# An attention and FP4 passage on one core: gates term by term, a fourth scaling buffer, earlier unpacking, and a reordered start

## The reference

```python
x = (h - mu) * rsqrt(var + EPS) * ln_g + ln_b
q, k, v = (x @ w.T + b for w, b in ...)        # 16 heads of 128, rope on q and k
attn = softmax(where(causal, -inf, q @ k.T * scale))
y = (attn @ v) @ wo.T + bo + residual
Wg, Wu, Wd = (LUT[4-bit codes] * scales per 32) # MLP 2048, the FP4 weights
gate, up = xt @ Wg.T, xt @ Wu.T
out = (gelu(gate) * up) @ Wd.T
```

## Time and profile before

| | before |
|---|---|
| median of 3 runs | 573.86 us (573.19 to 574.56) |
| profiled execution, its own time | 574.48 us |
| its span, first to last instruction | 572.7 us |
| busy: PE, DVE, ACT, POOL | 529.3, 472.8, 388.4, 389.3 us |
| granted clock of TensorE, mean | 0.994 |

### The profile page before, as it was taken

The page is one execution under the profiler, slowest core; times in us unless marked ns, Lnnn a source line. Parts: engine busy times, 40 slices in busy tenths (PEclk is TensorE's granted clock), DMA queues, the critical chain, the costliest instruction groups (busy, mean ns, idle before and its releaser), DMA issues.

```text
span 572.7 us, 11429 instructions
## 1 busy us (share of the span) xinstructions
PE 529.3 (92%) x4176; PEld 360.9 (63%) x4176; DVE 472.8 (83%) x875; ACT 388.4 (68%) x856; POOL 389.3 (68%) x351
## 2 busy tenths in 40 slices
PE   6768999999999999999997989899999989999894
PEld 2445666666666666766665555455688778656673
DVE  6899999999999999999998786576636986867656
ACT  5965879689787787778788576657676457557221
POOL 6877898899999899889897588622324453534442
PEclk9998999999999999999999999999999999999998
DMA  8235484646554335675355324112110000000002
GB/s 267 76 68 112 120 166 94 124 103 140 94 126 86 72 73 88 156 132 70 70 94 134 106 85 136 38 49 83 31 38 2 2 1 1 0 1 2 2 1 73
DMA packets 97880, 44.63 MB, mean 78 GB/s; under 512 B 87712, under 2 KB 90144, under 8 KB 97824
## 3 DMA queue, kind: packets, MB, share of 16 engines
q1 hardware_dynamic: 97392, 43.61, 33.5%
q10 hardware_dynamic: 432, 0.29, 0.2%
HBM read 21.86 MB, written 1.05 MB: 40 GB/s over the span
## 4 chain that ended last, share of the span: by engine, by line
PE 53%; DVE 22%; ACT 8%; POOL 7%; issue 6%; DMA 2%; SPq 1%; ACTq 0%; POOLq 0%; DVEq 0%
PE bank L1700 47%; PE bank L1887 4%; DVE turned L1244 3%; POOL qkl L647 2%; DVE parts L1267 2%; DVE nmax L1232 2%; DMA x<-in_x 2%; DVE stats L1114 1%; DVE turned L1475 1%; DVE stage L1516 1%; DVE ol L1281 1%; DVE w_all_l L1179 1%; DVE nrm L1127 1%; PE bank L1747 1%; ACT bank L838 1%
## 5 line engine op out<-in xcount | busy, mean ns | idle before, releaser
L1700 PE MATMUL bank<-xTh,w_all_h 128*128 128x512 f16 (+2 forms) x388 | 128.6, 331 | 12.3 <-DVE w_all_l L1179 3.6
L1700 PE MATMUL bank<-xTh,w_all_l 128*128 128x512 f16 (+2 forms) x388 | 128.5, 331 | 0.0
L1700 PE MATMUL bank<-xTl,w_all_h 128*128 128x512 f16 (+2 forms) x388 | 128.3, 331 | 0.0
L647 POOL TENSOR_TENSOR qkl<-turned,qkh 128x512 f16<-128x512 f32 (+1 forms) x44 | 55.4, 1260 | 96.0 <-ACT qkh L980 95.7
L571 POOL TENSOR_TENSOR rr<-turned 64x512 f32<-64x512 f32 x62 | 87.3, 1408 | 12.2 <-DVE turned L1244 8.3
L572 POOL TENSOR_TENSOR rr<-turned 64x512 f32<-64x512 f32 x62 | 82.2, 1326 | 3.6
L838 ACT ACTIVATE bank<-bank,nmax 128x128 f32<-128x128 f32 (+3 forms) x128 | 63.9, 499 | 29.8 <-DVE nmax L1232 29.0
L1244 DVE SCALAR_TENSOR_TENSOR turned<-bank,small,rope 128x1024 f32<-128x1024 f32 x64 | 81.1, 1269 | 0.6 <-PE bank L1768 0.6
L980 ACT ACTIVATE qkh<-turned 128x512 f16<-128x512 f32 (+1 forms) x44 | 27.6, 628 | 60.6 <-DVE turned L1475 60.6
L1267 DVE SCALAR_TENSOR_TENSOR parts<-bank,rscaled,parts 128x128 f16<-128x128 f32 (+3 forms) x128 | 64.3, 540 | 1.5 <-ACT parts L849 1.5
L1700 PEld LDWEIGHTS bank<-xTh,w_all_h 128*128 128x128 f16 (+1 forms) x388 | 37.9, 98 | 40.5 <-issue 11.0
(11 more groups left out here) (240 smaller groups left out, 1480.1 us busy)
## 6 DMA issues: line engine op xcount, KB each, us to landing
stage<-in_per_head SPq DMA_DIRECT2D x16, 512.0 KB, 4.3
xa<-in_codes SPq DMA_DIRECT2D x32, 128.0 KB, 2.8
stage<-in_packed SPq DMA_DIRECT2D x12, 256.0 KB, 3.0
stage<-in_scales SPq DMA_DIRECT2D x12, 256.0 KB, 3.5
pT<-parts SPq DMA_TRANSPOSE x128, 2.9
stage<-in_w1T SPq DMA_DIRECT2D x2, 512.0 KB, 4.7
rope<-in_ropes SPq DMA_DIRECT2D x1, 512.0 KB, 8.2
x<-in_x SPq DMA_DIRECT2D x1, 512.0 KB, 9.1
```

The costliest lines, as they stand in the source:

```text
L647: pool.tensor_tensor(il[n % 2][0:rows, :], inter[0:rows, n % 2, :], ih[n % 2][0:rows, :], ALU.subtract).then_inc(g_il, 1)
L1700: last = pe.matmul(dst, l, r, start=start and i == 0, stop=stop and i == 2, skip_group_check=skip)
```

## The change

- First heads. The norm of batch OTHER that the residual needs leaves `norms0`; its three instructions stand at steps 5, 6 and 7 (LATE_NORM_AT). GpSimd no longer waits for d_qkl ahead of its two weight halves, only ahead of the rotation. The copy of the turned x of OTHER into xT moves from VectorE to ScalarE (in `high_xT0`). VectorE makes the late weight half of a step ahead of `low_xT0`.
- Loads. Packed codes and scales are loaded apart; packed 4 to 7 at steps 25, 26, 28 and 29, scales 4 to 7 after the last `turn`. Bytes 4 and 5 are made at step 31.
- Passage. w32 has four buffers. VectorE copies the first 256 columns of piece 0 (`high_fp4_first`) at step 31, ScalarE the rest at step 32. TensorE makes gates 0 and 1 term by term at step 32 (`gates_high` ahead of `out_project(30)`, `gates_low` behind), then ups 0 and 1, and in step 33 gate 2, up 2 and gate 3; the loop over tiles begins with up 3. Pair 2 is unpacked ahead of `low_fp4(2)`, and `scaled(4)` and `scaled(5)` stand ahead of `low_inter(0)`. The later pieces stand at other tiles, and the shift and normal_x of batch FIRST one tile sooner.

The diff, cut (new semaphores, three-part `norm0`, signatures left out; all instructions that move are there):

```diff
@@ -37,7 +37,9 @@
...
 BYTES_AT = (23, 24, 25, 27)
+PACKED_AT = (25, 26, 28, 29)
 X0_TURN_AT = {0: 0, 1: 1}
+LATE_NORM_AT = (5, 6, 7)
@@ -54,9 +56,9 @@
...
 Q_PIECES = 3 * MLP // Q_COLS
-UNPACK_AT = {2: 3, 4: 4, 7: 5}
-SCALED_AT = {0: 4, 1: 5, 3: 6, 4: 7, 5: 8, 6: 9, 8: 10, 9: 11}
-HIGH_AT = {0: 3, 1: 4, 2: 5, 4: 6, 5: 7, 6: 8, 7: 9, 9: 10, 10: 11}
+UNPACK_AT = {1: 3, 4: 4, 6: 5}
+SCALED_AT = {2: 6, 3: 7, 4: 8, 6: 9, 7: 10, 8: 11}
+HIGH_AT = {0: 4, 1: 5, 3: 6, 4: 7, 5: 8, 7: 9, 8: 10, 9: 11}
@@ -196,7 +198,7 @@
...
-w32 = [rope, rr, turned[:, 1, 2:4, :]]
+w32 = [rope, rr, turned[:, 1, 2:4, :], turned[:, 1, 0:2, :]]
@@ -467,12 +472,17 @@
...
-    def load_fp4(j):
+    def load_packed(j):
+        w, cols = q_piece(j)
+        if j >= 4:
+            sp.wait_ge(a_byte, j - 3)
+        sp.dma_start(raw[:, j % 4, :], packed[w, :, cols]).then_inc(s_raw[j % 4], 16)
+
+    def load_scales(j):
...
             sp.wait_ge(g_w32, NIBBLES * (j - 3))
-        sp.dma_start(raw[:, j % 4, :], packed[w, :, cols]).then_inc(s_raw[j % 4], 16)
-        sp.dma_start(scl[:, j % 4, :], scales[w, :, cols]).then_inc(s_raw[j % 4], 16)
+        sp.dma_start(scl[:, j % 4, :], scales[w, :, cols]).then_inc(s_scl[j % 4], 16)
@@ -495,9 +505,6 @@
...
     for s in STEPS:
-        if s == UNITS - 1:
-            load_fp4(4)
-            load_fp4(5)
@@ -509,9 +516,17 @@
...
             for j in range(4):
-                load_fp4(j)
-    for j in range(6, Q_PIECES):
-        load_fp4(j)
+                load_packed(j)
+                load_scales(j)
+        if s in PACKED_AT:
+            load_packed(PACKED_AT.index(s) + 4)
+    for j in range(4, 8):
+        load_scales(j)
+    for j in (8, 10):
+        load_packed(j)
+        load_packed(j + 1)
+        load_scales(j)
+        load_scales(j + 1)
@@ -560,13 +575,19 @@
...
         pool.wait_ge(d_rope, 2 * u + 2)
+        if u - 2 == LATE_NORM_AT[0]:
+            pool.wait_ge(g_var0, 5)
+        if u - 2 == LATE_NORM_AT[1]:
+            pool.wait_ge(g_var0, 6)
+        if u - 2 == LATE_NORM_AT[2]:
+            pool.wait_ge(g_norm0, 3)
...
             pool.wait_ge(d_qkl, 2)
-            pool.wait_ge(g_norm0, 3)
+            pool.wait_ge(g_norm0, 2)
@@ -617,30 +641,31 @@
...
         norm0(1, OTHER, square0[:, :], (1.0 + LN_EPS) / D, LN_EPS ** 2)
-        norm0(2 + OTHER, OTHER, square0[:, :], 1.0 / D, LN_EPS)
...
         if s == 0:
-            pool.wait_ge(d_qkl, 2)
...
             low_qk(s + 1)
+        if s in LATE_NORM_AT:
+            norm0(2 + OTHER, OTHER, square0[:, :], 1.0 / D, LN_EPS, (LATE_NORM_AT.index(s),))
...
         pool.wait_ge(d_bits, 2 * (j // 2) + 2)
-        if j >= 3:
-            pool.wait_ge(d_fl, j - 2)
+        pool.wait_ge(s_scl[j % 4], 16 * (j // 4 + 1))
+        if j >= 4:
+            pool.wait_ge(d_fl, j - 3)
...
             code = bits_of(j // 2)[:, c, j % 2, :].bitcast(FP8)
-            pool.tensor_tensor(w32[j % 3][:, c, :], code, scl[:, j % 4, :], ALU.mult).then_inc(g_w32, 1)
+            pool.tensor_tensor(w32[j % 4][:, c, :], code, scl[:, j % 4, :], ALU.mult).then_inc(g_w32, 1)
@@ -677,7 +702,7 @@
...
     pool.wait_ge(g_qkl, lows_of(UNITS, 0) - 1)
-    for j in range(4):
+    for j in range(6):
         scaled(j)
@@ -801,7 +826,10 @@
...
         for c in cs:
-            act.wait_ge(d_xT, place(b) * KC + c + 1)
+            act.wait_ge(t_xT, place(b) * KC + c + 1)
+            act.activation(xT[:, c, :], acc_bank[c][:, :], ACT.Identity,
+                           scale=ln_g[:, c:c + 1], bias=ln_b[:, c:c + 1]).then_inc(a_xT, 1)
+            act.wait_ge(a_xT, c + 1)
@@ -881,6 +909,9 @@
...
             high_o(s - 2)
+        if s == UNITS - 1:
+            to_bytes(4)
+            to_bytes(5)
@@ -929,10 +960,15 @@
...
+    def high_fp4_rest():
+        act.wait_ge(g_w32, NIBBLES)
+        act.activation(fh[0][:, :, 2 * P:Q_COLS], w32[0][:, :, 2 * P:Q_COLS], ACT.Copy,
+                       scale=W_SCALE * FP4_AS_FP8).then_inc(a_fh, 1)
...
         act.wait_ge(g_w32, NIBBLES * (j + 1))
-        act.activation(fh[w][:, :, cols], w32[j % 3][:, :, :], ACT.Copy, scale=W_SCALE * FP4_AS_FP8).then_inc(a_fh, 1)
+        act.activation(fh[w][:, :, cols], w32[j % 4][:, :, :], ACT.Copy, scale=W_SCALE * FP4_AS_FP8).then_inc(a_fh, 1)
@@ -997,6 +1033,7 @@
...
             gate_of(0, ACT.Gelu_apprx_tanh)
+            high_fp4(3)
@@ -1004,20 +1041,16 @@
...
             high_xT(1, 0, (1,))
-            act.wait_ge(t_proj, 2 * UNITS)
-            high_fp4(0)
...
             act.wait_ge(t_v, UNITS)
+            high_fp4_rest()
...
     def between_first(m):
-        if m == 0:
-            to_bytes(4)
-            to_bytes(5)
...
             normal_y(0, 1)
-        if m == 11:
+        if m == 10:
             normal_x(0, 1)
@@ -1190,9 +1222,9 @@
...
     dve.wait_ge(d_vec, 1)
-    turned_x0(FIRST, (1,))
+    turned_x0(1)
     dve.wait_ge(a_xTh, 1)
-    turned_x0(FIRST, (0,))
+    turned_x0(0)
@@ -1307,11 +1339,9 @@
...
             rotated_first()
-        if s in X0_TURN_AT:
-            turned_x0(OTHER, (X0_TURN_AT[s],))
+        prepare(s, 1)
...
             low_xT0(OTHER, (X0_TURN_AT[s - 1],))
-        prepare(s, 1)
@@ -1349,8 +1379,17 @@
...
+    def high_fp4_first():
+
+        dve.wait_ge(t_proj, 2 * UNITS)
+        dve.wait_ge(g_w32, NIBBLES)
+        dve.tensor_scalar(fh[0][:, :, 0:2 * P], w32[0][:, :, 0:2 * P], W_SCALE * FP4_AS_FP8, None,
+                          ALU.mult).then_inc(d_fh, 1)
...
+        if s == UNITS - 1:
+            high_fp4_first()
@@ -1529,14 +1568,16 @@
...
         if s == UNITS:
+            dve.wait_ge(d_fh, 1)
...
             low_fp4(1)
+            dve.wait_ge(t_pv, UNITS - 1)
+            unpacked(2)
+            signed(2)
             low_fp4(2)
-    product_of(0)
+            product_of(0)
+            low_fp4(3)
     attention_sums()
-    dve.wait_ge(t_pv, UNITS - 1)
-    unpacked(2)
-    signed(2)
@@ -1555,7 +1596,7 @@
...
             spread_of_x(0, 1)
-        if m == 10:
+        if m == 9:
             shifted(0, 1, "x")
@@ -1829,20 +1870,52 @@
...
             turn_norm(1, 0, even_odd, (1,))
+        if s == UNITS:
+            gates_high()
         if s == UNITS + 1:
-            gate_up(0, fp4_weights(0), whole, beside_first, 0, (1,))
+            gate_up(2, fp4_weights(0), whole, beside_first, 4, (0,))
...
         if s == UNITS:
-            pe.wait_ge(d_pl, TPB * UNITS)
-            pe.wait_ge(d_xTl, (TURNS.index((1, 0)) + 1) * KC)
-            gate_up(0, fp4_weights(0), whole, beside_first, 0, (0,))
+            gates_low()
+            gate_up(0, fp4_weights(0), whole, beside_first, 0, (1,))
+            gate_up(1, fp4_weights(0), whole, beside_first, 2, (1,))
+        if s == UNITS + 1:
+            gate_up(2, fp4_weights(0), whole, beside_first, 4, (1,))
+            gate_up(3, fp4_weights(0), whole, beside_first, 6, (0,))
...
+
+    def gate_term(n, weights, c, x, start=False, stop=False):
+
+        return pe.matmul(G_bank[n][:, :], weights[:, c, n * P:(n + 1) * P], x[:, c, 0:S], start=start, stop=stop)
+
+    def gates_high():
+
+        turned = TURNS.index((1, 0)) * KC
+        pe.wait_ge(d_fh, 1)
+        pe.wait_ge(a_xTh, turned + KC)
+        for n in range(2):
+            pe.wait_ge(d_pl, TPB * (UNITS - 1) + n + 1)
+            gate_term(n, fh[0], 0, xTh, start=True)
+            gate_term(n, fh[0], 0, xTl)
+            gate_term(n, fh[0], 1, xTh)
+        pe.wait_ge(d_pl, TPB * UNITS)
+        pe.wait_ge(d_xTl, turned + KC)
+        for n in range(2):
+            gate_term(n, fh[0], 1, xTl)
+
+    def gates_low():
+
+        pe.wait_ge(d_fl, 1)
+        for n in range(2):
+            for c in range(KC):
+                last = gate_term(n, fl[0], c, xTh, stop=c == KC - 1)
+            last.then_inc(t_gate, 1)
@@ -2069,8 +2142,8 @@
...
     for m in range(M_TILES):
-        if m:
-            gate_up(RUN1 + m, fp4_weights(0), whole, beside_first, 2 * m)
+        if m >= 3:
+            gate_up(RUN1 + m, fp4_weights(0), whole, beside_first, 2 * m, (1,) if m == 3 else (0, 1))
```

More of the change, by code:

```diff
@@ L235, in sandwich @@
         s_raw = [sem(f"s_raw{i}") for i in range(4)]
+        s_scl = [sem(f"s_scl{i}") for i in range(4)]
         s_idx = [sem(f"s_idx{i}") for i in range(4)]
@@ L240, in sandwich @@
         a_fh = sem("a_fh")
+        d_fh = sem("d_fh")
         d_fl = sem("d_fl")
@@ L1162, in first_norm, with turned_x0 @@
                                       ALU.subtract, ALU.mult).then_inc(d_nrm0, 1)
-            def turned_x0(b, cs=range(KC)):
-                for c in cs:
-                    dve.wait_ge(t_xT, place(b) * KC + c + 1)
-                    dve.tensor_scalar(xT[:, c, :], (acc_bank if b == OTHER else T_bank)[c][:, :], ln_g[:, c:c + 1], ln_b[:, c:c + 1],
-                                      ALU.mult, ALU.add).then_inc(d_xT, 1)
+            def turned_x0(c):
+                dve.wait_ge(t_xT, c + 1)
+                dve.tensor_scalar(xT[:, c, :], T_bank[c][:, :], ln_g[:, c:c + 1], ln_b[:, c:c + 1],
```

(3 more changed lines are left out.)

20 lines of the change are left out of this document (12 added, 8 removed).

## The result

The changed kernel takes **571.21 us** (median of 5 runs, 570.92 to 571.87). The kernel before, beside it, took 573.86 (5 runs, 573.19 to 574.56). The ratio is **0.9946** with a 95% interval of 0.9931 to 0.9961, so some 3.1 us are gone (2.2 to 4.0). The forecast was 570.6, faster. The profiled execution took 570.92, its span is 569.1 us.

What follows compares the result with a forecast made beforehand. TensorE bounds the kernel, busy 529.3 of 572.7 us, so only its 43 us of standing can be won. Heads -0.9, passage -2.0 and look-up -0.4 sum to -3.3, taking the median 573.86 to 570.6 us, range 567.0 to 573.6.

Steps and rivals of the forecast that it cites:

- The clash: First heads: GpSimd's sooner weight halves alternate with VectorE's qkl pair, delaying all of head 1 by 1.6 us.
- Copies on ScalarE: First heads: VectorE loses two xT copies of 0.7 us, -1.4; ScalarE hides them in its waits.
- Order on VectorE: First heads: VectorE's weight half goes ahead, meeting GpSimd's rotation better; -0.5 at step 0, -0.6 at step 1.
- my rule: VectorE two-input and GpSimd SBUF instructions share one port pair; whichever starts first holds it for the whole instruction.
- Late norm: Heads: the norm's power returns at step 6 ahead of a rotation, covered by GpSimd's waits; 0, upper bound 0.5 us.
- Wait of 2.08 filled: Passage: matmuls of gates 0 and 1 with fh[0] fill TensorE's wait for ol of the last head but one, -2.1.
- its price in the passage: Passage: waits that come late next, found by walking four queues, give back +5.8 us of the 7.8 won.
- the 2.4 forecast: Passage's forecast gain: -2.0 us by the turn of x and -0.4 at the second look-up.
- the stretch behind it: Turn of x to second look-up: half of the 0.77 us wait for one-hot tiles at 391.5 goes, -0.4.
- Kept fed: Rival, chance 0.22: no clash at 18.5 us and only half of the passage's given-back waits; 568.1 us.
- Moved waits: Rival, chance 0.12: the passage's waits reappear whole, only the heads' -0.9 is left; 573.0 us.
- GpSimd held by the scales: Rival, chance 0.08: in the passage scales 4 land late, low_inter(0) is delayed and TensorE held; 575.4 us.

Runs made afterwards that it cites:

- Run 12: Run 11's kernel with GpSimd's start again waiting for VectorE's first pair of low halves: 568.28 us, ratio 0.9895 to the kernel before.
- run 11: Changed kernel with high halves of FP4 tiles 6 to 8 one step later and scales 4 and 5 loaded ahead of the last transposes: 570.50 us, ratio 0.9934.
- run 9: Changed kernel with GpSimd again waiting at the start for VectorE's first pair before the weights' low halves, late norm kept: 569.98 us, ratio 0.9925.
- Run 6: Changed kernel with the two copies of the turned x back on VectorE, behind the weights' low half: 572.37 us, ratio 0.9963.
- Run 5: Changed kernel with VectorE in steps 1 and 2 again taking the turned x's low half ahead of the weights' low half: 571.76 us, ratio 0.9945.
- run 2: Changed kernel with the first heads as before, so the passage's edits alone: 573.05 us, ratio 0.9977 to the kernel before.
- run 3: Changed kernel with GpSimd's start as before, both the third norm and the wait for VectorE's subtractions: 571.31 us, ratio 0.9941.
- run 8: Changed kernel with the scales of FP4 tiles 4 and 5 loaded ahead of unit 31's transposes: 571.35 us, ratio 0.9937.
- run 1: Kernel before with the change's edits to the first heads alone: 572.43 us, ratio 0.9954.
- run 10: Changed kernel with only the third norm back at GpSimd's start instead of steps 5 to 7: 569.83 us, ratio 0.9928.

## Why the prediction was right, and where it was wrong

The total of -3.3 us was right (-3.1 by the ratio). Several of its terms were not, and it took luck for them to cancel.

- **The clash, +1.6: right.** The rotation began at 24.18 (forecast 24.4), VectorE's pair took 3.14, scores(0) was 1.69 late. Over all profiles it stands at 20.88 to 22.62 in the eight with the new start and at 19.92 to 20.47 in the six without it, medians 1.8 apart. Run 12 against run 11 gained 2.2 us by taking the clash away; run 9 gained 1.2, with overlapping intervals.
- **Copies on ScalarE, -1.4: right in size.** Run 6: 1.0 to 1.2 us in time. ScalarE took them for nothing that shows.
- **Order on VectorE, -0.5 and -0.6: wrong.** The failed step is "it would be 0.65 and, behind a GpSimd instruction of 1.65, another 1.65". I took it from two rows in which a lone subtraction met GpSimd, and here two of them stand back to back. One such pair was in the trace before, at step 2 (53.90 and 54.50), and it went by my rule. But where the first one was ahead of GpSimd in step 1, the second took 0.68 in eight of eleven profiles, and GpSimd paid (2.25). In the table that is the larger part of the 3.79 us at scores(4), where my terms give 0.9. Run 5 shows further that the order by itself is worth nothing; by the rows, what counts in step 1 is that no copy stands ahead of both subtractions, and either of two edits sees to that.

  The 5.5 us that the profiles gain between scores(0) and scores(4) divide so. From scores(2) to scores(3) it took 12.61 us before, 11.79 in run 2, 10.33 in runs 3 and 8, where GpSimd went between the subtractions, and 9.07 after: 2.7 us for step 1, its copy included, at the full clock, and the other 0.8 goes with the lower clock of the profile before. From scores(3) to scores(4) it took 9.98 before, 9.28 after, and 9.36 in run 2, where the second subtraction of step 2 took 0.69 and not 1.76: 0.7, of which 0.6 is that clash. The rest, 1.2, lies between scores(0) and scores(2), where the first copy was. So some 1.4 of the 5.5 us, the clock and the clash in step 2, are chance of the one profile before, since run 2 has neither there in the same order; the 2.6 us of run 1's time are the better figure for the heads.
- **Late norm, 0 with 0.5 as the bound: its bound.** The cover I named at step 7 was not enough: TensorE waits 0.65 at 93.08, and run 10 gets 0.5 us back.
- **Wait of 2.08 filled: right; its price in the passage: near; the stretch behind it: wrong in sign.** The waits of the earlier trace rows went as forecast, and the largest new ones stand where the walk of the queues put them: 1.51 at down(4), where 1.3 was forecast, and 1.10 at down(8), where 1.0 was. What was given back by the turn of x is 6.6 instead of 5.8, and then came what the sum had with the wrong sign: "VectorE is ahead by about as much as TensorE, so I give half of 0.77: -0.4". So of the 2.4 forecast 0.8 were lost by the turn of x and 1.1 behind it. TensorE waited more there, and the stretch from turn to look-up grew by 0.73 (19.19 against 18.46). The profile before and after, for that stretch:

```profile
373.04:391.50 18.46, 17.69 (x109) 10.78 (x110) 15.47 (x32) 11.07 (x21) 5.23 (x4) 1.00 0.22 63
```

```profile
368.75:387.94 19.19, 17.92 (x110) 10.49 (x109) 15.10 (x33) 11.22 (x21) 7.78 (x5) 1.00 0.23 65
```

  GpSimd has 7.78 us in it instead of 5.23: a part of its work now lies behind the turn of x, and TensorE came there sooner than its partners.
- **The rivals.** *Kept fed* fell on its first condition, the clash. *Moved waits* comes nearest to what the passage did (0.4 to 1.1 us kept in the profiles, 1.3 by run 2's time); it was paid for by the heads. *GpSimd held by the scales*: GpSimd did wait 5.34 us, but TensorE not at all for low_inter(0), and run 8 gains nothing in the passage by taking it away.

The forecast's two errors, -2.2 in the heads and +2.0 in the passage by the profiles (-1.7 and +1.1 by the times of runs 1 and 2), have opposite signs. A right total is weak evidence for its terms; the two halves run apart showed it.

## What to carry to other kernels

Edits in queues that feed each other are not terms of a sum: the early gates were worth 2.7 us in the new order of VectorE, and without them that order won nothing in the passage and lost some, so run the halves apart, and judge a passage at the last wait behind it, not at the first mark that moved. When an instruction is taken out of a queue, look at what starts sooner behind it: here a norm of 2 us was the spacer that kept two engines' subtractions apart, and one wait, on an engine that stands anyway, was worth 2.2 us. A short VectorE copy out of a bank, ahead of subtractions that read two tiles, can cost more than its length where GpSimd is about to start: 2.7 us in step 1 for a copy of 0.8. And a single pair of profiles is one draw: look at a second profile of the same code before a difference is called the change's.
